# A gated context product and a BitNet feed-forward on one core: opening, first products, weight rounding, passage and drain rearranged

## What is computed

```python
def xattn(h, token_ids, Wg, Wu, Wd):            # Wg = Wu = Wd = ctx_2048
    for e in range(4):
        g = silu(einsum('bsd,fd->bsf', h, Wg[e])); u = einsum('bsd,fd->bsf', h, Wu[e])
        y = einsum('bsf,df->bsd', g * u, Wd[e])
        out = where((expert_ids == e)[..., None], y, out)

def ffn(x, w_gate, w_up, w_down):               # w_gate, w_up 2048x512, w_down 512x2048
    gate, up = bitlinear(x, w_gate), bitlinear(x, w_up)
    return h_bitlinear(silu(gate) * up, w_down) # a Walsh-Hadamard transform over 2048 comes first
# bitlinear: x to 8-bit integers by its row's absmax, w to -1, 0, 1 by its mean |w|

x = x + tanh(g_xattn[0]) * xattn(layernorm(x), ids, ctx, ctx, ctx)
x = x + tanh(g_ffn[0]) * ffn(layernorm(x), w_gate, w_up, w_down)
```

## Time and profile before

| | |
|---|---|
| median of three runs | 443.35 us (442.98 to 445.31) |
| the profiled execution | 442.68 us, span 440.6 us |
| TensorE busy | 401.6 us (91%) |
| VectorE busy | 378.0 us (86%) |
| ScalarE busy | 290.4 us (66%) |
| GpSimd busy | 180.1 us (41%) |
| mean granted TensorE clock | 0.983 |

### The profile page before, as it was taken

One profiled execution on the slowest core, in us unless ns is written; L12 is line 12 of the kernel. 1 busy time (PEld: TensorE's weight loads), 2 busy tenths in 40 slices (PEclk: granted clock), 3 DMA queues, 4 the chain that ended last, 5 costly groups with the idle time before them and its releaser, 6 DMA issues.

```text
span 440.6 us, 7506 instructions
## 1 busy us (share of the span) xinstructions
PE 401.6 (91%) x2251; PEld 277.8 (63%) x2252; DVE 378.0 (86%) x645; ACT 290.4 (66%) x447; POOL 180.1 (41%) x211
## 2 busy tenths in 40 slices
PE   1889999999999788799999999999999999999971
PEld 0358787878878533465656666666666666667820
DVE  5795799689869879899999999999999999999540
ACT  4524654864784453458778878878888787877820
POOL 0627401101110405365655765576585566421010
PEclk9999999999999989899999999999999999999987
DMA  7687323405410000322462453355245247424430
GB/s 290 235 292 260 102 95 123 165 0 191 135 57 0 2 13 10 61 60 38 84 121 60 83 119 89 67 107 120 48 107 119 62 82 120 99 59 107 97 104 27
DMA packets 50999, 44.16 MB, mean 100 GB/s; under 512 B 44833, under 2 KB 44833, under 8 KB 48929
## 3 DMA queue, kind: packets, MB, share of 16 engines
q1 hardware_dynamic: 46256, 27.63, 22.6%
q0 software_dynamic: 4720, 16.26, 15.8%
HBM read 21.33 MB, written 4.19 MB: 58 GB/s over the span
## 4 chain that ended last, share of the span: by engine, by line
PE 72%; DVE 12%; issue 5%; DMA 5%; POOL 3%; ACT 2%; SPq 0%; DVEq 0%; POOLq 0%; ACTq 0%
PE bank L437 20%; PE bank L501 11%; PE bank L508 11%; PE bank L532 10%; PE bank L525 10%; PE bank L401 8%; DMA xqT<-xq 2%; DMA stage<-ctx_dram 2%; DVE ct_lo L877 2%; DVE prod L1146 1%; DVE prod L1160 1%; POOL xs L292 1%; PE bank L573 1%; DVE stage L1111 1%; DVE ymax_part L1126 1%
## 5 line engine op out<-in xcount | busy, mean ns | idle before, releaser
L501 PE MATMUL bank<-wq,xqT 128*128 128x512 bf16 x256 | 67.5, 387 | 4.2 <-DMA xqT<-xq 4.2
L525 PEld LDWEIGHTS bank<-cst,mT 128*128 128x128 f32 x480 | 62.6, 192 | 11.9 <-issue 2.3
L532 PE MATMUL bank<-wq,yqT 128*128 128x512 bf16 x256 | 66.1, 385 | 3.4 <-DMA yqT<-yq 3.4
L508 PE MATMUL bank<-wq,xqT 128*128 128x512 bf16 x256 | 67.4, 387 | 1.1 <-DVE prod L1146 1.1
L525 PE MATMUL bank<-cst,mT 128*128 128x128 f32 x480 | 63.5, 275 | 1.7 <-ACT mT L738 1.7
L763 ACT ACTIVATE sg<-bank,gate_s 128x512 f32<-128x512 f32 x64 | 43.7, 683 | 14.1 <-PE bank L501 11.7
L384 POOL DMA_INDIRECT out_dram<-res,order x16 | 19.5, 1216 | 76.4 <-DVE res L1166 76.4
L1146 DVE TENSOR_TENSOR prod<-bank,sg 128x512 f32<-128x512 f32 x64 | 43.3, 678 | 4.8 <-PE bank L508 4.4
L726 ACT ACTIVATE y<-y,yqs 128x512 int8<-128x512 f32 x56 | 40.2, 717 | 10.2 <-POOL yqs L352 10.2
L738 ACT ACTIVATE mT<-bank 128x512 f32<-128x512 f32 x60 | 35.4, 593 | 17.3 <-PE bank L401 17.3
L508 PEld LDWEIGHTS bank<-wq,xqT 128*128 128x128 bf16 x256 | 25.4, 99 | 32.8 <-issue 2.2
(11 more groups left out here) (148 smaller groups left out, 865.2 us busy)
## 6 DMA issues: line engine op xcount, KB each, us to landing
mixed<-mixed POOLq DMA_DIRECT2D x15, 512.0 KB, 5.2
stage<-ctx_dram SPq DMA_DIRECT2D x4, 1024.0 KB, 10.4
stage<-wgate_dram SPq DMA_DIRECT2D x4, 1024.0 KB, 7.6
stage<-wup_dram SPq DMA_DIRECT2D x4, 1024.0 KB, 4.8
stage<-wdown_dram SPq DMA_DIRECT2D x4, 1024.0 KB, 4.7
yqT<-yq SPq DMA_TRANSPOSE x64, 2.4
cst<-consts_dram SPq DMA_DIRECT2D x1, 338.0 KB, 3.3
xs<-x_dram,order POOLq DMA_INDIRECT x16, 3.8
```

Source lines behind the costliest of these rows:

```text
L501: last = nc.tensor.matmul(ps_gate[:, :], xqT[:, b, c, :], wq[:, 0, c * F + 512 * n:c * F + 512 * (n + 1)], start=(c == 0), stop=(c == DC - 1))
L508: last = nc.tensor.matmul(ps_up[n % 2][:, :], xqT[:, b, c, :], wq[:, 1, c * F + 512 * n:c * F + 512 * (n + 1)], start=(c == 0), stop=(c == ...
L525: last = nc.tensor.matmul(bank_[:, c * P:(c + 1) * P], mT[:, n % 2, c, :], had, start=True, stop=True)
L532: last = nc.tensor.matmul(ps_down[b][:, :], yqT[:, m, g, :], wq[:, 2, block_ * D:(block_ + 1) * D], start=(m == 0 and g == 0), stop=(m == ...
```

## The change

It edits every stage but the feed-forward's loop.
- The constants come in two DMAs, the two matrices for ranking first and in bf16; the ranking steps are fewer, `pick_tile` is written ahead of the cast of `lo_i`, `pick_row` column block by column block; ScalarE makes `pick_part` before it rounds contexts. Three gathers, not four, precede the first `item_scale`. There are fewer spins.
- The up products of items 0 and 1 multiply float32 by float32 (4 matmuls each, straight from `stage`), without remainders. The first down product waits for all four `ct_lo`. The loads of the first weight matrix wait for both.
- The items are written out. ScalarE scales a weight chunk and writes 8-bit integers (`w8`), VectorE clips them into `wq` in one pass, and the schedule has five items for a matrix.
- Layer norm and quantising of feed-forward tiles 0 and 1 happen within items 16 to 18. The down product of item 18 comes after the first quarter of tile 0.
- In the drain all Hadamards precede the down quarters of tile A, the residual add of A comes after the integers of C, and C is transposed on TensorE instead of by DMA.

```diff
-C_ID, C_H, C_TRI, C_ONE, C_IOTA = 0, P, 2 * P, 3 * P, 4 * P
+C_TRI, C_SUM, C_RANK = 0, P // 2, P
+C_IOTA, C_ID, C_H, C_ONE = P, 2 * P, 3 * P, 4 * P
+FIRST = 2
+        w8 = (xn2[:, 0, :].bitcast(I8), xn2[:, 1, :].bitcast(I8),
+              xq[:, :, :].bitcast(I8).rearrange("p a n -> p (a n)"))
+        xT_whole = wq[:, 0, 0:2 * D].bitcast(F32)
+        ps_down_last, ps_yT = bank[0], (bank[2], bank[5], bank[3], bank[4])
         @block.sync
-            sp.dma_start(cst[:, :], consts).then_inc(in_small, 16)
+            sp.dma_start(cst[:, 0:C_RANK], consts[:, 0:C_RANK]).then_inc(in_rank, 16)
+            sp.dma_start(cst[:, C_RANK:C_N], consts[:, C_RANK:C_N]).then_inc(in_small, 16)
...
                     if w == 0:
                         sp.wait_ge(ct_lo_set, c + 1)
+                        sp.wait_ge(h_done, FIRST)
                     else:
-                        sp.wait_ge(wq_set, 4 * (w - 1) + c + 1)
+                        sp.wait_ge(wround_set, 4 * (w - 1) + c + 1)
...
-            for t in (NT - 2, NT - 1):
-                for m in range(NQ):
-                    turn_y(t, m)
+            for m in range(NQ):
+                turn_y(NT - 2, m)
         @block.tensor
+            def first_product(k):
+                e = expert_of(k)
+                pe.wait_ge(ct_hi_set, e + 1)
+                pe.wait_ge(xT_hi_set, k + 1)
+                if k >= 1:
+                    pe.wait_ge(act_set, k)
+                for c in range(DC):
+                    last = nc.tensor.matmul(ps_h[:, :], xT_whole[:, c * P:(c + 1) * P],
+                                            stage[:, ds(e), c * D:(c + 1) * D], start=(c == 0), stop=(c == DC - 1))
+                last.then_inc(h_done, 1)
...
-            spin(24)
+            spin(18)
             pe.wait_ge(stats_set, 1)
             spin(5)
             x_transposes(0, 0)
-            spin(6)
+            spin(4)
             pe.wait_ge(tables_set, 1)
-            up_product(0, 0, first=True)
+            first_product(0)
             x_transposes(1, 1)
-            spin(14)
+            spin(4)
             a_transposes(0)
...
+                if k == 1:
+                    pe.wait_ge(ct_lo_set, E)
                     down_product(k - 1)
...
                         if isinstance(t, int) and t == 0 and n == 1:
-                            pe.wait_ge(aT_lo_set, NI)
+                            down_product(NI - 1, ps_y_last)
                         gate_up(t, b, n)
...
-                down_product_int(A, A % 2, 1)
                 pe.wait_ge(y_set, B * NQ + 4)
                 last_hadamard(1)
-                down_product_int(A, A % 2, 2)
                 for p in range(2, 4):
                     pe.wait_ge(y_set, C * NQ + p - 1)
                     last_hadamard(p)
-                down_product_int(A, A % 2, 3)
-                for t in (B, C):
-                    pe.wait_ge(res_set, t - 1)
-                    for m in range(NQ):
-                        down_product_int(t, t % 2, m)
+                for m in range(1, NQ):
+                    down_product_int(A, A % 2, m)
+                pe.wait_ge(res_set, B - 1)
+                down_product_int(B, B % 2, 0)
+                down_product_int(B, B % 2, 1)
+                y_transposes(0)
+                y_transposes(1)
+                down_product_int(B, B % 2, 2)
+                y_transposes(2)
+                down_product_int(B, B % 2, 3)
+                y_transposes(3)
+                for m in range(NQ):
+                    pe.wait_ge((yT_dve_set, yT_act_set)[m % 2], m // 2 + 1)
+                    for g in range(4):
+                        block_ = (m + 2) % NQ * 4 + g
+                        last = nc.tensor.matmul(ps_down_last[:, :], yT_end[:, m, g, :],
+                                                wq[:, 2, block_ * D:(block_ + 1) * D],
+                                                start=(m == 0 and g == 0), stop=(m == 3 and g == 3))
+                last.then_inc(down_done, NQ)
         @block.scalar
             def weight_round(w, c):
-                act_e.wait_ge(wclip_set, w * 4 + (c + 1))
-                act_e.wait_ge(ct_hi_set, E)
-                nc.scalar.activation(wq[:, ds(w), c * F:(c + 1) * F].rearrange("p a n -> p (a n)"),
-                                     stage[:, c, :], ACT.Copy, bias=-MAGIC).then_inc(wq_set, 1)
+                j = 4 * w + c
+                act_e.wait_ge(wscale_set, w + 1)
+                if j >= 3:
+                    act_e.wait_ge(wq_set, j - 2)
+                nc.scalar.activation(w8[j % 3], stage[:, c, :], ACT.Copy,
+                                     scale=wscale[:, w:w + 1]).then_inc(wround_set, 1)
         @block.vector
+            def weight_clip(w, c):
+                j = 4 * w + c
+                dve.wait_ge(wround_set, j + 1)
+                ts(wq[:, w, c * F:(c + 1) * F], w8[j % 3], 1.0, -1.0, ALU.min, ALU.max).then_inc(wq_set, 1)
...
             def row_picks(half):
-                own = slice(NT // 2 * half, NT // 2 * (half + 1))
-                tt(pick_row[:, own, :], iota_bf[:, :].unsqueeze(1).to_broadcast([P, NT // 2, P]),
-                   lo_f[:, own].unsqueeze(2).to_broadcast([P, NT // 2, P]), ALU.is_equal).then_inc(picks_set, 1)
+                for t in range(NT // 2 * half, NT // 2 * (half + 1)):
+                    last = ts(pick_row[:, t, :], iota_bf[:, :], lo_f[:, t:t + 1], None, ALU.is_equal)
+                last.then_inc(picks_set, 1)
...
                 for p in range(NQ):
-                    if p == 2:
-                        finish(A, A % 2)
                     dve.wait_ge(y_set, C * NQ + p + 1)
...
                 for m in (0, 2):
                     y_integers(C, c, m)
+                finish(A, A % 2)
+                for m in (0, 2):
+                    dve.wait_ge(yT_done, m + 1)
+                    nc.vector.tensor_copy(yT_end[:, m, :, :].rearrange("p g t -> p (g t)"),
+                                          ps_yT[m][:, :]).then_inc(yT_dve_set, 1)
```

More of the change, by code:

```diff
@@ L305, in item_scale @@
                 return n + 1
-            for t in range(4):
+            for t in range(3):
                 gather(t)
@@ L310, in _ @@
             n = item_scale(1, n)
-            gather(4)
-            gather(5)
+            for t in range(3, 6):
+                gather(t)
             n = item_scale(2, n)
@@ L1028, in _ @@
             normalise(2, 0)
+            ct_lower(3)
             def ln_stats(t, b, s):
@@ L1116, in _, with weight_scale @@
-            for w in range(3):
-                round_(w, st, last=w == 2)
-            dve.wait_ge(wq_set, 11)
+            def weight_scale(w):
+                own = slice(w, w + 1)
+                dve.wait_ge(wsum_done, w + 1)
+                st.did(nc.vector.tensor_reduce(wsum[:, own], ps_wsum[:, 0:4], AX_X, ALU.add))
+                st.wait()
+                st.did(ts(wmean[:, own], wsum[:, own], 1.0 / (D * F), Q_EPS, ALU.mult, ALU.max))
+                st.wait()
+                nc.vector.reciprocal(wscale[:, own], wmean[:, own]).then_inc(wscale_set, 1)
@@ L1207, in body @@
                     if gu:
-                        late = isinstance(t, int) and t == 1
-                        if late and n == 1:
+                        multiply(t, b, n)
+                        if isinstance(t, int) and t == 0 and n == 1:
                             update(NI - 1, ps_y_last)
-                            multiply(t, b, 0)
-                        if not (late and n == 0):
-                            multiply(t, b, n)
                     if ln and n == 1:
```

312 lines of the change are left out of this document (159 added, 153 removed).

## The result

| | before | after |
|---|---|---|
| median | 443.17 us (442.41 to 445.31, 4 runs) | 436.54 us (435.58 to 437.4, 4 runs) |
| profiled execution | 442.68 us, span 440.6 | 435.58 us, span 433.8 |
| TensorE, VectorE busy | 401.6, 378.0 us | 395.5, 363.3 us |

The account below looks back on a forecast made before the run. TensorE bounds the kernel except in the opening, passage and drain; 1.5 + 0.9 + 5.1 + 4.1 = 11.6 us off the profiled 442.68 gives 431.1, forecast 431.5 us, range 427.5 to 436.

Parts of the forecast that it names:

- the items written out: From item 2 to the last down product: gaps at the loop's turn and one chunk wait go, 0.9 us, bounds 0 and 1.2.
- the drain: After the last Hadamards: integers start sooner, last residual add at 427.9 instead of 431.97, 4.1 us, bounds 2.5 and 4.7.
- The opening: Up to item 2's up product: start at 38.0 instead of 39.47, 1.5 us, bounds 0.2 and 3.5.
- the passage: From item 18 into the feed-forward: first butterfly 4.4 us sooner, item 18's update leaves tile 1, 0.7; 5.1 us, bounds 3.5 and 6.
- The first evacuation: ScalarE's first transposed x in the opening: 20.5 us instead of 22.67, after gathers landing in 3.8 us and the last context.
- the new chain: Opening behind the first evacuation: full product, remainders, down product, transposes, lower part; 17.5 us until item 2 starts.
- the opening gives nothing: Rival: low clock slows the first full product to up to 7 us, or gathers and contexts delay each other; loses 2 to 5 us; 0.13.
- the rest of the ramp keeps its VectorE work and shifts whole: Passage behind the first butterflies, up to 226 us: the work moves earlier unchanged, so the passage's 5.1 us is kept.
- GpSimd steps: Rival: VectorE's ramp up to 226 us hangs on something unseen, such as these, swallowing the 5 us: 436 us; 0.04.
- The largest rival: Weights come late or the 8-bit pass is slow; TensorE waits, 2 to 4 us back, 433.5 to 435.5 us; 0.17.
- VectorE's pass from 8-bit: Weight chunks: one pass from 8-bit to bf16 takes 1.23 us, replacing two of 1.23 to 1.28, hidden by TensorE.
- the first butterfly: Passage: start at 161.9 on the old clock instead of 166.28, near 159.5 in the changed kernel.

Follow-up runs that it names:

- a0: The changed kernel run again unaltered: 437.75 us, ratio 0.9891 against the kernel before.
- two groups of repairs: Changed kernel with only the opening's edits, 433.03 us; changed kernel with only the passage's (tile 2 statistics early, layer-norm passes behind SiLU, fourteen idle matmuls), 433.67 us.
- the opening's repairs: Changed kernel with register read first, item 2's transposes first, 24 and 8 idle matmuls: 433.03 us, ratio 0.9783 against before.
- all repairs: Changed kernel with the opening's and the passage's edits together, idle matmuls included: 430.67 us, ratio 0.9733 against before.
- e1a: Changed kernel with VectorE taking tile 2's layer-norm statistics one quarter of a tile earlier: 435.80 us, ratio 0.9837 against before.
- e13: Changed kernel with tile 2's statistics early, layer-norm passes behind the SiLU of items 17 and 18, fourteen idle matmuls in the ramp: 433.67 us, ratio 0.9802 against before.

## Why the prediction missed

The direction was right and two terms out of four hold: the items written out (0.9, seen as 1.0 at the transposes behind item 17) and the drain (4.1, measured 3.9). The opening and the passage failed. The drain alone gives what could be measured of the whole change.

*Opening, 1.5 us forecast, 0.3 in the first profile and 2 lost in the typical one.* The first evacuation came near its figure (20.23 in the first profile, 19.93 to 21.86 in the ten) by luck, since it hangs on the first gather, priced at 3.8 us, a median over sixteen, and taking 5.4 to 6.4 in the two chains read, and not on the contexts. From there to the end of the last remainder it took 12.73 us (12.9). The step that failed is what follows in "the new chain". It left out the register read behind the wait (0.8) and the times from one engine to the next between transposes and up product (2.17 us, where 1.74 were counted), and it took the down product at full clock in all cases: 1.6 us in eight of ten profiles. (The parts as listed also add to 17.7, not to 17.5.) The rival "the opening gives nothing" named the granted clock behind a wait. In four of the ten the clock was low where it said, but the full product took 3.60 to 4.11 us and not near 7. The place with the larger and commoner loss was the down product behind the wait for the last remainder. I gave the rival 0.13, having counted that the idle matmuls go from 24 to 18 and from 14 to 4, but not asked how long TensorE stands after them.

*Passage, "the rest of the ramp keeps its VectorE work and shifts whole".* It did not. From U to S 5.1 us were to be gained by the passage, with 3.5 as the lower bound, beside the 0.9 of the items. After taking off 1.0 for the items, the first profile has 1.7 and `a0` 3.1. Between G and S 1.1 to 2.9 us were gone (165.73 to 167.54 where 164.6 was laid out). The removed wait had been a shelter, in which two of GpSimd's three steps got through. Without it all three meet two-operand passes of VectorE in SBUF, take 5.1 us instead of 3.1, and ScalarE is queued behind them, and TensorE behind ScalarE (3.87 us). This is the mechanism of the rival "GpSimd steps", to which I gave 0.04, though the passage did not lose all 5 us by it, as the rival had it. It is shown by two edits of opposite kind, work moved ahead and a wait added. The Trainium skill (SBUF — State Buffer, the section "SBUF: two separate sides") says that GpSimd and VectorE share one pair of ports, and that whichever starts first, an instruction of GpSimd or one of VectorE with two SBUF inputs, holds it for the whole instruction while the other stands. The trace agrees: a step that otherwise takes 0.26 us takes 2.41, the length of two such passes (2.36).

*Items 17 and 18.* The layer-norm passes were priced at nothing, inside the items. They stand in ScalarE's stream ahead of the SiLU and cost 1.5 us, which is why the gates came 0.95 us later after U than laid out. I had listed the time they need and not what is queued behind them.

*Weights.* The largest rival (0.17) did not come. The loads of the first matrix took 10.7 us (median of four), TensorE did not wait at its sum, and VectorE's pass from 8-bit took 1.22 (I took 1.23).

*Drain.* It came as laid out, with the last residual add 8.7 us before the end of the span (I said 8.6) and the clock at 1.00 in the last down product. The Trainium skill's figure (TensorE: Matmul & The Clock Gate, part 4) would have made the sixteen transposes 4.4 us, an estimate; it is given there for TensorE's transpose mode, and this kernel issues plain matmuls against an identity. The chain has 0.45 + 0.22 + 0.22 for the sixteen, half of the 0.11 each that I had taken from float32 ones. The measurement decides.

The two groups of repairs show that both places cost time. They do not divide the miss of 5 us exactly, since the opening's repairs (U at 36.57 and 36.13) go beyond what was forecast (37.7). So it is in part chance that the kernel with all repairs lands on the forecast time. What remains open: why the clock holds in some executions and falls in others with gaps of like length, how much of the kernel's spread (some 1%) comes from it, and why G to S scatters by up to 1.8 us between profiles of the same code.

## What to carry to other kernels

A wait that is removed may have been the time in which a third engine got through: look for what ran in it, and for what stands in order behind that. When work is moved into a busy stage, the cost is in the queue behind it and not in its own duration. And where TensorE's idle time is only moved, ask at which clock it comes back; here idle matmuls, a register read ahead of its wait and one set of transposes moved turned an opening that typically lost 2 us into one that gained 2.7 and 3.1 in the two profiles of it. And a mark that is forecast is to be compared on one clock, counted from a mark ahead of it: the first butterfly at 161.89 looked like a hit, and was 2.4 us late.

## What was not expected of the hardware

- GpSimd operations on 128 x 1 elements take 0.19, 0.55 and 0.26 us alone, and 1.12, 1.41 and 2.41 us beside VectorE's two-operand float32 passes.
- A register read by TensorE behind a semaphore wait cost some 0.8 us in which nothing ran (1.00 us from release to matmul, and 0.23 with the read ahead of the wait); the chain calls it "issue".
- A stretch at the lower clock need not cost anything: G to S took 164.70 us with clocks of 0.65 and 0.50 in the 8 us from 176 (`e1a`), and 164.63 with 1.00 throughout (`e13`).
